# Cross-attention weights: low halves made from high halves that TensorE puts into PSUM, and context values without a doubled copy of the context

## The reference

```
xn1 = _ln(x, g1, be1)
sa = _mha(xn1, xn1, Wq_s, bq_s, Wk_s, bk_s, Wv_s, bv_s, causal=True)
x = x + (sa @ W1 + b1)
xn2 = _ln(x, g2, be2)
ca = _mha(xn2, encoder_out, Wq_c, bq_c, Wk_c, bk_c, Wv_c, bv_c, causal=False)
x = x + (ca @ W2 + b2)
xn3 = _ln(x, g3, be3)
ff = jax.nn.relu(xn3 @ Wf1 + bf1) @ Wf2 + bf2
...
q = jnp.einsum('btc,hcd->bhtd', xn, Wq) + bq[None, :, None, :]
k = jnp.einsum('bsc,hcd->bhsd', kv_src, Wk) + bk[None, :, None, :]
v = jnp.einsum('bsc,hcd->bhsd', kv_src, Wv) + bv[None, :, None, :]
scores = jnp.einsum('bhtd,bhsd->bhts', q, k) / scale
attn = jax.nn.softmax(scores, axis=-1)
out = jnp.einsum('bhts,bhsd->bhtd', attn, v)
```

## Time and profile before

| | us |
|---|---|
| median of 3 runs | 2360.87 (2355.35 to 2362.05) |
| profiled execution | 2361.88 |
| its span in the trace | 2360.1 |
| mean granted TensorE clock, share of full | 0.972 |

### The profile page before, as it was taken

How to read it: one execution, slowest core, us unless ns; L and a number is a source line. 1 busy time by engine, 2 the same in 40 slices (tenths; PEclk the granted TensorE clock), 3 DMA queues, 4 the chain that set the end, 5 groups by cost and what they waited for, 6 DMA issues and landing times.

```text
span 2360.1 us, 31416 instructions
## 1 busy us (share of the span) xinstructions
PE 2204.9 (93%) x11206; PEld 1602.3 (68%) x11206; DVE 1414.2 (60%) x3349; ACT 867.1 (37%) x1598; POOL 933.5 (40%) x943
## 2 busy tenths in 40 slices
PE   6999999999999999788999998999999999999996
PEld 4665565556555655446777776788887887888784
DVE  4378757775677576835666668553446445464546
ACT  3145545554555455433334334321112122121213
POOL 1057766766677576864333333110111202021212
PEclk9899999999999999799999999999999999999998
DMA  7265545554555446221211112321112111211011
GB/s 232 30 87 96 100 66 83 96 96 67 81 98 91 73 74 119 68 72 62 82 54 59 54 60 87 109 90 40 37 67 72 54 64 53 94 54 67 32 36 49
DMA packets 106320, 177.29 MB, mean 75 GB/s; under 512 B 18334, under 2 KB 23454, under 8 KB 106160
## 3 DMA queue, kind: packets, MB, share of 16 engines
q1 hardware_dynamic: 106164, 175.29, 32.0%
HBM read 83.67 MB, written 40.13 MB: 52 GB/s over the span
## 4 chain that ended last, share of the span: by engine, by line
PE 75%; DVE 9%; issue 6%; ACT 4%; POOL 3%; DMA 2%; SPq 0%; POOLq 0%; ACTq 0%; DVEq 0%
PE psum L55 18%; PE psum L56 17%; PE psum L57 17%; PE psum L797 5%; PE psum L745 5%; PE psum L785 4%; PE psum L806 2%; PE psum L703 1%; DVE psum L1000 1%; DMA small<-es 1%; ACT sx L1346 1%; POOL es L660 1%; PE psum L1300 1%; PE psum L1241 1%; PE psum L1292 1%
## 5 line engine op out<-in xcount | busy, mean ns | idle before, releaser
L660 POOL TENSOR_TENSOR es<-es,er 128x512 f32<-128x512 f32 (+3 forms) x640 | 589.2, 956 | 336.8 <-PE psum L797 297.7
L895 ACT ACTIVATE er<-psum 128x512 f32<-128x512 f32 (+3 forms) x640 | 279.7, 470 | 319.5 <-DVE psum L1011 186.2
L1000 DVE CUSTOM_DVE_ANT_0 psum<-psum,mask_ts 128x384 f32<-128x384 f32 (+3 forms) x512 | 248.0, 500 | 220.2 <-PE psum L745 219.3
L745 PE MATMUL psum<-ks,qs 96*128 96x512 f32 (+3 forms) x768 | 269.5, 376 | 20.8 <-DMA ks<-stage 10.8
L785 PE MATMUL psum<-qs,ks 100*128 100x512 f32 (+3 forms) x768 | 261.5, 373 | 20.9 <-DVE mx L1004 9.5
L1850 ACT ACTIVATE fy<-psum,cols 128x512 f32<-128x512 f32 x128 | 88.2, 689 | 451.9 <-PE psum L57 451.3
L745 PEld LDWEIGHTS psum<-ks,qs 96*128 96x128 f32 x768 | 144.8, 196 | 120.6 <-issue 46.7
L1004 DVE TENSOR_REDUCE mx<-psum 128x1 fp32r<-128x512 f32 x256 | 175.1, 684 | 63.8 <-PE psum L745 63.0
L785 PEld LDWEIGHTS psum<-qs,ks 100*128 100x128 f32 x768 | 144.4, 194 | 93.3 <-DVE mx L1004 24.4
L55 PE MATMUL psum<-fh,hh 128*128 128x512 f32 x512 | 201.0, 393 | 7.1 <-DVE hl L1951 7.1
L55 PE MATMUL psum<-fah,fh 128*128 128x512 f32 x512 | 202.8, 396 | 0.0
(11 more groups left out here) (258 smaller groups left out, 4497.4 us busy)
## 6 DMA issues: line engine op xcount, KB each, us to landing
qs<-stage SPq DMA_DIRECT2D x96, 256.0 KB, 5.7
ks<-stage SPq DMA_DIRECT2D x96, 256.0 KB, 6.8
rs<-rs_d SPq DMA_DIRECT2D x32, 256.0 KB
sa_d<-rs SPq DMA_DIRECT2D x32, 256.0 KB, 2.1
sx<-sa_d SPq DMA_DIRECT2D x8, 1024.0 KB, 5.6
xt<-in_x SPq DMA_DIRECT2D x32, 256.0 KB, 6.0
x_d<-xt SPq DMA_DIRECT2D x32, 256.0 KB, 2.0
fw<-in_Wf SPq DMA_DIRECT2D x16, 512.0 KB, 5.4
```

What stands on the lines that cost most here:

```text
L660: e.tensor_tensor(es, es, er, ALU.add).then_inc(s_add.sem, 1)
L745: t = e.matmul(bank1(*s)[:, v * wd:v * wd + wd], Q.qs[par][0:96, i, 128 * ti:128 * ti + 128], Q.ks[par][0:96, i, c0:c0 + wd], start=True, ...
L895: e.activation(dst, bank1("sc", g, c2, j, i)[:, off:512], ACT.Exp, scale=SCALE).then_inc(s_freeS.sem, 1)
L1000: t = e.tensor_tensor_reduce(out=ps, in0=ps, in1=mask_ts[:, 512 - wd:512], scale=1.0, scalar=-3e38, op0=ALU.add, op1=ALU.max, accum_out=mx ...
```

## The change

Three things.

1. A new step 2wm (j, k) on TensorE, between 2wh and 2wl: the high half is multiplied by the identity into a bank, and 2wl subtracts from the raw weight what stands in that bank, where before it read the high half from SBUF. banks1 gives these twelve uses banks, free 0.02 after their 2wl; so all uses behind them get other banks too.
2. 2cd and its semaphore are gone.
3. 2cv multiplies the context itself, 64 positions as weights, once for even heads into rows 0 to 63 and once for odd heads into rows 64 to 127, each with 256 columns of Wv_c (32 of every 64). 2cve reads 256 adjacent columns.

```diff
+        elif s[0] == "2wl":
+            ends["2wm", *s[1:]] = at + 0.02
...
-                             (15.03, ("2z", 1)), (14.9, ("2cd",)))]
+                             (15.03, ("2z", 1)))]
...
-            t += [(at + 0.04 * k, ("2wh", j, k)), (at + 0.04 * k + 0.05, ("2wl", j, k))]
+            t += [(at + 0.04 * k, ("2wh", j, k)), (at + 0.04 * k + 0.025, ("2wm", j, k)), (at + 0.04 * k + 0.05, ("2wl", j, k))]
...
+            elif use[0] == "2wm":
+                w.wait_ge(s_wl2, 4 * use[1] + use[2] + 1)
...
+            elif s[0] == "2wm":
+                _, j, k = s
+                free1(w, *s)
+                w.wait_ge(s_wh2, 4 * j + k + 1)
+                e.matmul(bank1(*s), identr[:], R.W[("W1", "Wq_c", "W2")[j]][0][:, k, :], start=True, stop=True).then_inc(s_wm2.sem, 1)
...
                 freeK(w, 5 + b)
-                w.wait_ge(s_cd, 8)
+                w.wait_ge(d_ct2, 16)
                 w.wait_ge(d_wk2, 128)
                 for k in range(KT):
-                    at = 512 * (k % 2) + 128 * b
-                    t = e.matmul(bank[(5 + b) % 2], cd[k // 2][:, at:at + 128], R.wkv[:, k, :], start=k == 0, stop=k == 3)
+                    for j in range(2):
+                        t = e.matmul(bank[(5 + b) % 2][64 * j:64 * j + 64, 0:256], R.ct[:, k, S * b:S * b + S],
+                                     R.wkv[:, k, :].rearrange("p (h j d) -> p j h d", j=2, d=DH)[:, j], start=k == 0, stop=k == 3)
...
-                Wh, Wl = R.W[("W1", "Wq_c", "W2")[j]]
-                src = R.raw[j % 2][:, k, :]
-                w.wait_ge(s_wh2, 4 * j + k + 1)
+                Wl = R.W[("W1", "Wq_c", "W2")[j]][1]
+                src, hi = R.raw[j % 2][:, k, :], bank1("2wm", j, k)
+                w.wait_ge(s_wm2, 4 * j + k + 1)
                 if j == 1:
-                    e.scalar_tensor_tensor(Wl[:, k, :], src, col("g2", k), Wh[:, k, :].bitcast(F32),
-                                           ALU.mult, ALU.subtract).then_inc(s_wl2.sem, 1)
-                else:
-                    e.tensor_tensor(Wl[:, k, :], src, Wh[:, k, :].bitcast(F32), ALU.subtract).then_inc(s_wl2.sem, 1)
+                    e.scalar_tensor_tensor(Wl[:, k, :], src, col("g2", k), hi, ALU.mult, ALU.subtract).then_inc(s_wl2.sem, 1)
+                else:
+                    e.tensor_tensor(Wl[:, k, :], src, hi, ALU.subtract).then_inc(s_wl2.sem, 1)
...
-            elif s[0] == "2cd":
-                w.wait_ge(d_ct2, 16)
-                stacked(w)
-                for k in range(KT):
-                    for j in range(2):
-                        dst = cd[k // 2][:, 512 * (k % 2):512 * (k % 2) + 512].rearrange("p (b j s) -> p b j s", j=2, s=S)
-                        e.tensor_copy(dst[:, :, j, :], R.ct[:, k, :].rearrange("p (b s) -> p b s", s=S)).then_inc(s_cd.sem, 1)
```

More of the change, by code:

```diff
@@ L1049, in program @@
         R.nm, R.sm = [small[:, p, 40:56] for p in range(2)], [small[:, p, 72:88] for p in range(2)]
-        cd = [q[:].rearrange("p h s -> p (h s)") for q in R.pp]
         R.useI, R.useT = {}, {}
@@ L1063, in program @@
         d_x2 = [[sem(f"d_xs{p}{i}") for i in range(4)] for p in range(3)]
-        s_wh2, s_wl2, s_z2, s_cd, s_kh, s_kl, s_vb = (sem(n) for n in ("s_wh2", "s_wl2", "s_z2", "s_cd", "s_kh", "s_kl", "s_vb"))
+        s_wh2, s_wl2, s_z2, s_kh, s_kl, s_vb = (sem(n) for n in ("s_wh2", "s_wl2", "s_z2", "s_kh", "s_kl", "s_vb"))
+        s_wm2 = sem("s_wm2")
         s_wb2, s_bw2, s_fillK = sem("s_wb2"), sem("s_bw2"), sem("s_fillK")
@@ L1418, in dve2 @@
                     r = slice(64 * j, 64 * j + 64)
-                    o, i0, i1 = (q.rearrange("p (h j d) -> p h j d", j=2, d=DH)[:, :, j, :]
-                                 for q in (R.vb[r, b, :], bank[(5 + b) % 2][r, :], bvc[r, :]))
-                    e.tensor_tensor(o, i0, i1, ALU.add).then_inc(s_vb.sem, 1)
+                    o, i1 = (q.rearrange("p (h j d) -> p h j d", j=2, d=DH)[:, :, j, :] for q in (R.vb[r, b, :], bvc[r, :]))
+                    e.tensor_tensor(o, bank[(5 + b) % 2][r, 0:256].rearrange("p (h d) -> p h d", d=DH), i1, ALU.add).then_inc(s_vb.sem, 1)
             elif s[0] == "2sl":
```

## The result

The changed kernel takes 2363.64 us (median of 20 runs, 2351.82 to 2370.45), the kernel before 2359.51 us beside it (20 runs, 2354.4 to 2363.84). The ratio is 1.0021, 95% interval [1.0011, 1.0030]: slower by about 5 us, where 8 us faster were forecast. The time lies 2.6 us above the upper end of the range. Each kernel has one trace: how often a wait that it shows comes in other executions is not known.)

The account below looks back on a forecast made before the run. TensorE was 93% busy, but the touched stretch waited through transfers, VectorE, copies and value products. Terms: -4.9 us at 1011 us, -2.0 and -1.5 for the value groups, -8.4 in all; forecast 2352.5 us, range 2348 to 2361.

Parts of the forecast that it names:

- step 8: Behind the first value group: of 4.8 us from the other three, 1.5 counted; the shift then stays to the end.
- rival D: First al lands in GpSimd's unbroken adds from 1017.45 and waits to near 1042.6; -0.5, 2360.4 us; chance 0.13.
- rival C: The 9.84 us of the first Wq_cl don't hang on the operand; -5.8, 2355.1 us; chance 0.06.
- Step 1: Before the Wq_c transfer: W1l falls from 1.83 to 0.68 us, so the transfer issues earlier; -1.0 us.
- Step 2: First Wq_cl loses its 9.1 us wait, but VectorE's work restarts only 2.6 us earlier, W1l's gain included.
- Step 3: Up to 984 us: eight copies gone, -3.2 us; the two middle Wq_cl shorter, -0.6 us for both.
- Step 5: 980 to 988 us: without the copies' idle time TensorE should reach full clock; -1.0 us, bounds 0 and -4.
- Step 6: Key products: W2's four transfers stand ahead of or between them on TensorE; +1.5 us, bounds 0 and +3.
- Step 7: 1011 to 1052 us: value groups by halves take 3.4 us (first) and 1.8; -2.0 and three times -1.6.
- Rival B: Value products: halves don't overlap or TensorE stands still at width changes; groups unchanged, -4.9, 2356.0 us; chance 0.10.
- Rival E: Twelve transfers bind TensorE's queue to ScalarE, 1.7 us each; +9.5, 2370.4 us; chance 0.06.
- Rival A: Shift partly eaten as transfers hold PSUM banks until late in VectorE's queue; -4.7, 2356.2 us; chance 0.17.

Follow-up runs that it names:

- values alone: Kernel before with only the value products by 64-column halves and no copies; low halves still from two SBUF operands: 2357.77 us, ratio 1.0000.
- Low halves alone: Kernel before with only the low halves made from high halves in PSUM; copies and old value products stay: 2360.40 us, ratio 1.0009.
- rows of adds alone: Four kernels without the computation, only rows of GpSimd adds with VectorE instructions asked for beside them: no VectorE instruction over 1.8 us in 120 rows.
- ah in PSUM: Changed kernel, and TensorE also puts ah of chunk 0 into PSUM, so each al has one SBUF operand: 2350.72 us, ratio 0.9968.
- the second part alone with either cure: Kernel before with value products by halves and no copies, plus a gap in GpSimd's adds (2350.30 us, 0.9971) or ah through PSUM (2351.36 us, 0.9971).

## Why the prediction was wrong

The step that failed, and put the kernel on the slow side, is the end of step 8: "nothing else changes. So the shift stays to the end." The first al, which the sum moved without a price, took 12.68 us instead of 1.82 and gave the whole gain back. That is rival D, at a price of 5 us more than it had. Ahead of it the shift at 1011 us was mis-sized too.

**Steps 1 to 4 (-5.4 up to 984 us)** came to -3.6 at the last Wq_cl. The 9.84 us wait is gone, and rival C with it. Step 1's -1.0 did not come: W1l fell to 0.68 us as expected, but VectorE waited for TensorE's maxima instead, and the transfer of Wq_c is issued 10.06 us behind the first W1h in both kernels. Step 2 nearly held: the maximum behind the first Wq_cl starts 24.5 us behind the first W1h, where it started at 26.7, so 2.1 of the 2.6 us came. **Step 3 (-3.2 - 0.6)** held for the copies alone (values alone are 3.4 us ahead at the last Wq_cl) but not on top of step 2. Low halves alone are 2.1 us ahead there, and both parts only 3.6: VectorE, rid of both, waits for TensorE, first behind the bias products and then again:

```profile
963.83 0.70 DVE L1004 CUSTOM_DVE_ANT_0 psum<-psum,mask_ts 128x512 f32<-128x512 f32 x1 [5.64 <-PE psum L749]
...
973.18 0.70 DVE L1004 CUSTOM_DVE_ANT_0 psum<-psum,mask_ts 128x512 f32<-128x512 f32 x1 [1.86 <-PE psum L749]
```

The prediction asked of the sum whether GpSimd allows it; the next bound was TensorE, at half clock for most of 958 to 988 us.

**Step 5 (-1.0 for the clock)** had the wrong sign. The granted clock of 972 to 988 was 0.50, and the first key products cost 3.20 us for 1.89. In values alone they took 1.95 us, nearly all at full clock:

```profile
984.00:992.00 8.00, 6.51 (x40) 4.13 (x39) 4.87 (x12) 6.68 (x18) 6.41 (x8) 1.00 0.01 2
```

**Step 6 (+1.5, bounds 0 and +3)** was the right mechanism and, within its bounds, the right size: 1.3 to 3 us. **Steps 1 to 6** together gave -0.7 at the first value products, where -4.9 stood; -4.9 is, of the terms that the sum has, the one mis-sized by most.

**Step 7 (groups of 3.4 and 1.8 us)** was right: 2.79 and 1.88. Halves of the array's columns run side by side, also with a moving operand that takes 32 of every 64 columns. The Trainium skill's rule that a change of tiling mode drains TensorE (page "TensorEngine Tiling (Array Packing)", section "Key Properties") has no price here that shows: 16 instructions took 1.88 us, and eight pairs at half of 0.43 us are 1.72, so at most 0.16 us a group is left for it. Rival B fell.

**Step 8** counted 3.5 us of the value part and took the rest as lost on GpSimd. From the first value products to the first al the changed kernel gained 6.0 us and values alone 7.8 us (table), where the four groups were costed at 6.8: about all of it arrived at the al. And there rival D decided: the al stood in the row of adds. Its mechanism and place were as written. That the moment agrees, GpSimd dry at 1043.02 for 1042.6 predicted, is luck: this execution was 2.83 us early from the first W1h on. Counted from there the last es add of the row ended 6.5 us earlier than in before (102.5 us for 108.9), not 8.4; one more add (L670, 1.25 us) stood behind it, and the al ended 0.55 us behind that. These are 3.7 of the 5 us by which D's price (-0.5) was too low. Its chance, 0.13, was the real error of the prediction. What spoke against it was that L1196 adds let al in at each boundary in the trace of before. But those adds had just started behind an idle time of 1.11 us, while the same view had Wq_cl shut out by an unbroken row of adds. The two rows were both there, and the place to which the al would move was like the second. That being in an unbroken row is the whole condition is not shown: in rows of adds alone VectorE got in each time.

**Rival E** had no part in it by its price: no transfer but W2's shows on the table. **Rival A**, partial losses ahead of the values, did happen; the clock and the overlap of the two gains are shown, a part of the banks is not.

**The sum** comes near once the stall is out: -8.4 us predicted, -7.5 us measured with ah in PSUM (0.9968 of 2358.09), and -6.8 us for the second part alone with either cure. That is luck in part: with ah in PSUM the shift at the first value products is -0.4 us for -4.9 predicted, and from there on 5.5 us are won up to the first al and 7.4 up to the last product with W1l, where steps 7 and 8 let 3.5 through. An error of 4.5 us and one of 2 to 4 us the other way nearly cancel.

## What to carry to other kernels

When an edit makes an instruction of VectorE with two SBUF operands earlier, look at what GpSimd does at its new time, not at its old one. If it lands in an unbroken row of adds, give the row one gap there, or bring one operand in through PSUM; neither showed a cost at four places (0.9971 with either in the second part alone), and a wait at every add costs far more than the stalls. Two waits on one engine that end at the same next bound were worth little more than the larger here (3.6 us for 3.4 and 2.1), not the sum: ask what the stage would look like with either gone before adding them, and ask it of every engine.

## What the runs showed of the hardware

A VectorE instruction with two SBUF operands, or a small one from SBUF, lost up to ten boundaries in a row to GpSimd's adds in these kernels (12.79 us at most; the small ones three, 4.70 us at most). In each of ten traces of whole kernels with plain rows one or two of the sixteen tensor_scalar of the layer norm waited 4 us and more; the rows of the two first kernels:

```profile
L973 DVE TENSOR_SCALAR small<-small x16: 157/166/4060, 6.9 to 728.8; 128x2 f32<-128x2 f32 x16
```

```profile
L977 DVE TENSOR_SCALAR small<-small x16: 156/166/4604, 6.7 to 724.7; 128x2 f32<-128x2 f32 x16
```

It falls on the first of the four of the second, third or fourth sequence, near 214, 444 or 672 us, and on another one or two of these three from trace to trace; the other thirteen took 0.17 us or less. Each such wait is longer than the others by some 4 us; whether it shifts what follows is not shown. I read the spread of the runs of one kernel (2352 to 2370 us) as in part made of such events, but that is argued, not shown. The Trainium skill, page "SBUF — State Buffer", section "Who interferes with whom", says of VectorE's two-port modes that whoever issues first holds the shared pair for the whole instruction and the other is blocked. The 120 rows of adds alone agree with a hold of one instruction (nothing over 1.8 us); in the kernels the waits are longer than one, and what is different in them none of these runs found.
